# One block of attention products and sums per chunk, and chunk 0 through the same projection as the others, in a fused gated cross-attention and int8 feed-forward kernel

## What is computed

```
x = x + tanh(g_xattn) * ( softmax( q k^T / sqrt(32) ) v  @ Wo.T + bo )
        q = layernorm(x) @ Wq.T + bq         16 heads of 32
        k = ctx @ Wk.T + bk,  v = ctx @ Wv.T + bv
h  = gelu( qlinear(layernorm(x), w1, b1) )   512 -> 2048, int8 with one scale per tensor
x  = x + tanh(g_ffn) * qlinear(h, w2, b2)    2048 -> 512
```

## Time and profile before

| | |
|---|---|
| median of three runs | 603.9 us |
| the profiled execution | 603.55 us, its span 601.8 us |
| PE (TensorE matmul) busy | 577.0 us, 96% |
| DVE (VectorE) / ACT (ScalarE) / POOL busy | 457.9 (76%) / 338.7 (56%) / 246.5 us (41%) |
| granted TensorE clock over the run | 0.994 of full |

### The profile page before, as it was taken

One profiled execution on the slowest core, in us unless ns is written; L12 is line 12 of the kernel. 1 busy time (PEld: TensorE's weight loads), 2 busy tenths in 40 slices (PEclk: granted clock), 3 DMA queues, 4 the chain that ended last, 5 costly groups with the idle time before them and its releaser, 6 DMA issues. The chain is left out here.

```text
span 601.8 us, 9279 instructions
## 1 busy us (share of the span) xinstructions
PE 577.0 (96%) x3320; PEld 329.7 (55%) x3320; DVE 457.9 (76%) x658; ACT 338.7 (56%) x412; POOL 246.5 (41%) x211
## 2 busy tenths in 40 slices
PE   6999899999998999999999988999999999999997
PEld 5853656657566566585664763444444454444443
DVE  5865997868869788696795786889998799945182
ACT  1556274573763836628346536778776778445440
POOL 3268366464651764916062410000004529313383
PEclk8999999999999999999999999999999999999999
DMA  9926010320411403202001159677777967789766
GB/s 307 402 90 211 14 49 10 105 106 1 176 35 35 177 0 131 81 13 95 0 1 71 71 191 379 261 282 288 271 270 307 420 228 263 296 333 356 230 252 209
DMA packets 41223, 105.57 MB, mean 175 GB/s; under 512 B 3168, under 2 KB 3936, under 8 KB 36576
## 3 DMA queue, kind: packets, MB, share of 16 engines
q1 hardware_dynamic: 39840, 103.70, 46.6%
q10 hardware_dynamic: 1344, 1.37, 0.8%
HBM read 63.11 MB, written 41.94 MB: 175 GB/s over the span
## 5 line engine op out<-in xcount | busy, mean ns | idle before, releaser
L1466 PE MATMUL ps<-h_sb,w_q 128*128 (+1 forms) x488 | 111.3, 383 | 2.7 <-ACT xo L1533 2.6
L1765 PE MATMUL ps<-w_q,h_q 128*128 128x512 bf16 x448 | 96.9, 379 | 0.0
L1848 POOL TENSOR_TENSOR xo<-xo,b2s 128x512 f32<-128x512 f32 x32 | 52.6, 1675 | 70.8 <-DMA xo<-x_dram 52.7
L1466 PEld LDWEIGHTS ps<-h_sb,w_q 128*128 128x128 bf16 x488 | 46.9, 99 | 55.8 <-ACT xo L1533 3.9
L1765 PEld LDWEIGHTS ps<-w_q,h_q 128*128 128x128 bf16 x448 | 43.8, 98 | 52.9
L1533 ACT ACTIVATE xo<-ps,b1s,sc 128x1024 f32<-128x1024 f32 x48 | 57.7, 1205 | 26.0 <-PE ps L1466 17.9
L715 ACT ACTIVATE q_hi<-ps,bq_sb 128x512 fp32r<-128x512 f32 x32 | 22.0, 688 | 83.5 <-DVE ps L945 77.4
L729 ACT ACTIVATE prob<-ps 77x1024 f32<-77x1024 f32 x64 | 61.7, 1014 | 12.2 <-PE ps L474 12.2
L1633 DVE TENSOR_REDUCE hmax<-xo 128x1024 f32 (+1 forms) x48 | 57.1, 1213 | 7.8 <-ACT xo L1533 7.7
L1194 POOL TENSOR_TENSOR xt_lo<-xr,xt_hi 128x512 fp32r<-128x512 f32 x28 | 35.8, 1298 | 54.8 <-ACT xt_hi L708 54.7
L1825 DVE SCALAR_TENSOR_TENSOR xo<-ps,hs,xo 128x512 f32<-128x512 f32 x32 | 23.3, 746 | 40.7 <-POOL xo L1848 40.7
(11 more groups left out here) (187 smaller groups left out, 1118.2 us busy)
## 6 DMA issues: line engine op xcount, KB each, us to landing
h_dram<-xo SPq DMA_DIRECT2D x48, 512.0 KB, 2.8
h_sb<-h_dram SPq DMA_DIRECT2D x16, 1024.0 KB, 11.2
x_dram<-x SPq DMA_DIRECT2D x8, 1024.0 KB, 4.5
xo<-x_dram SPq DMA_DIRECT2D x8, 1024.0 KB, 4.9
x<-h_dram SPq DMA_DIRECT2D x8, 1024.0 KB, 7.9
x<-in_x SPq DMA_DIRECT2D x7, 1024.0 KB, 5.8
xr<-in_x_t SPq DMA_DIRECT2D x28, 256.0 KB, 2.9
out<-xo SPq DMA_DIRECT2D x7, 1024.0 KB, 8.4
```

The lines of the kernel that those rows point to most:

```text
L1466: mm = nc.tensor.matmul(ps[:, 2 * (m % 2) + s, :], w1_q[:, k, m * P:(m + 1) * P], xq_t[:, one(2 * j + s), k, :], start=(k == 0), stop=(k = ...
L1765: mm = nc.tensor.matmul(ps[:, 4 * s + t, :], h_q[s][:, m, t * P:(t + 1) * P], w2_q[:, m, :], start=(m == 0), stop=(m == MF - 1))
L1848: nc.gpsimd.tensor_tensor(xo[:, s, t, :], xo[:, s, t, :], b2s[:], ALU.add).then_inc(xb_on, 1)
```

## The change

Two parts.

**Chunk 0.** `normalize1`, `transposes`, `first_high`, `first_low` and the eight mean products are gone. TensorE starts with the column means, four products in plain float32 on the raw `Wq`; VectorE subtracts them straight from PSUM (`centre_wq`), and chunk 0 is projected like the others, from four loaded slices of transposed x in `xt0_raw`, first slices 0 and 1 for all four m, in banks 4 to 7. `split_k` and `split_wo` move from VectorE to POOL, the early loads are spread over SyncE's and ScalarE's queues, the idle turns ahead fall from 30 to 10. The load of w1 waits until the four `xt_lo` of chunk 0 are done.

**Chunks 1 to 6.** `SLOTS` is 8, and the products and sums of a whole chunk stand in step i+1 between `project_q(i+1, 0)` and `project_q(i+1, 1)`. In the last step the old order stays. `scores_by_key(i, 3)` moves behind the first 8 products of output tile 1. On ScalarE the four `c_copy` of the chunk stand around `q_high(i, 0)`; `centre2(i-2, 0)` moves from the end of the step before to behind them, beside `centre2(i-2, 1)`; `round_w1` comes next. On VectorE `amax2(i-2, 0)` and `(i-2, 1)` stand behind `q_low(i, 0)`, ahead of `reciprocals(i-1)`.

```diff
-SLOTS = 4
+SLOTS = 8
 @block.tensor
+                    for k in range(KD):
+                        pe.wait_ge(wq_in[k], 16)
+                        mm = nc.tensor.matmul(ps[:, MEAN_BANK, :], mean_w[:].to_broadcast([P, P]), wq_raw[:, k, :],
+                                              start=(k == 0), stop=(k == KD - 1))
...
                 def first_step():
...
+                    for k in range(2):
+                        for m in range(KD):
+                            first_q(m, [k])
+                    first_q(0, [2])
+                    for m in range(GROUPS):
+                        project_k(m)
+                    first_q(0, [3])
+                    row_turn(0)
+                    first_q(1, [2, 3])
+                    pe.wait_ge(k_split_hi, 4)
                     scores_by_token(0, 0)
+                    first_q(2, [2, 3])
+                    project_v(0, range(KD // 4))
                     scores_by_token(0, 1)
...
                 def step(i):
...
                     project_q(i, 0)
-                    values(i - 1, GROUPS - 1)
-                    sums(i - 1, GROUPS - 1)
+                    if in_one_block(i - 1):
+                        for g in range(GROUPS - 1):
+                            values(i - 1, g)
+                            sums(i - 1, g)
+                        sums(i - 1, GROUPS - 1)
+                        values(i - 1, GROUPS - 1)
+                    else:
+                        values(i - 1, GROUPS - 1)
+                        sums(i - 1, GROUPS - 1)
                     project_q(i, 1)
...
                     scores_by_key(i, 1)
-                    values(i, 0)
-                    sums(i, 0)
+                    if i == LAST:
+                        values(i, 0)
+                        sums(i, 0)
                     if older:
                         pe.wait_ge(x1_on, TT * (i - 2) + 3)
-                    project_out(i - 1, 0, 0, 3)
+                    project_out(i - 1, 0, 0, 3 if i == LAST else 9)
                     scores_by_key(i, 2)
...
-                    project_out(i - 1, 1, 0, 6 if i == LAST else ALL)
-                    values(i, 2)
-                    sums(i, 2)
+                    if i == LAST:
+                        project_out(i - 1, 1, 0, 6)
+                        values(i, 2)
+                        sums(i, 2)
+                    else:
+                        project_out(i - 1, 1, 0, 8)
+                        scores_by_key(i, 3)
+                        project_out(i - 1, 1, 8, ALL)
...
-                idle_turns(nc, sh, BS, 30)
-                transposes(0)
-                transposes(1)
-                project_k(0)
...
+                weight_means()
+                pe.wait_ge(ident_in, 16)
+                idle_turns(nc, sh, BS, 10)
 @block.scalar
...
-                    if c or p >= SLOTS:
-                        act.wait_ge(sum_mm, GROUPS * c + p // 2 - 1)
+                    if c and p == 0:
+                        act.wait_ge(sum_mm, GROUPS * c)
+                        act.wait_ge(av_mm, GROUPS * c)
...
+                    if in_one_block(i - 1):
+                        c_copy(i - 1, 0)
+                    q_high(i, 0)
+                    for g in range(1 if in_one_block(i - 1) else GROUPS - 1, GROUPS):
+                        c_copy(i - 1, g)
                     if older:
+                        centre2(i - 2, 0)
                         centre2(i - 2, 1)
+                    if 2 <= i < 2 + KD:
+                        round_w1(i - 2)
+                    for m in range(1, KD):
+                        q_high(i, m)
...
+                    exponentials(i, 6)
+                    exponentials(i, 7)
                     if older:
                         centre2(i - 2, 2)
                         centre2(i - 2, 3)
-                    exponentials(i, 6)
-                    exponentials(i, 7)
-                    centre2(i - 1, 0)
-                    c_copy(i, 2)
 @block.vector
...
                 def step(i):
                     older = i >= 2
-                    if older:
-                        amax2(i - 2, 1)
                     q_scale(i, 0)
                     q_low(i, 0)
+                    if older:
+                        amax2(i - 2, 0)
+                        amax2(i - 2, 1)
                     reciprocals(i - 1)
...
-                    if older:
-                        amax2(i - 2, 2)
-                        amax2(i - 2, 3)
                     if i == 1:
                         w1_scale()
...
-                    amax2(i - 1, 0)
+                    if older:
+                        amax2(i - 2, 2)
+                        amax2(i - 2, 3)
+                    if i == LAST:
+                        amax2(i - 1, 0)
```

More of the change, by code:

```diff
@@ L198, in attention @@
         idents_on = sem("idents_on")
+        mean_w_on = sem("mean_w_on")
+        xt0_in = [sem(f"xt0_in{k}") for k in range(KD)]
         k_zeroed = sem("k_zeroed")
@@ L294, in row_bank @@
         def row_bank(n):
-            return BS if n == 1 else BC
+            return (ROW0_BANK, W1)[n] if n < 2 else BC
         def rec_wide(g):
@@ L302, in rstd_value, with xt_tile @@
         def rstd_value(c):
-            return c + 2
+            return c + 1
+        def xt_tile(n, k):
+            return xr[:, k % 2, :] if n else xt0_raw[:, k, :]
         def xr_value(n, k):
@@ L384, in _ @@
             def _(pe):
[L385 to L391, removed]
                 def row_turn(n):
@@ L397, in row_turn @@
                         pe.wait_ge(c_on, GROUPS * (n - 1))
+                    elif n == 1:
+                        pe.wait_ge(v_on, B)
                     for t in range(TT):
@@ L1052, in first_step @@
                 def first_step():
+                    q_scale(0, 0)
                     q_low(0, 0)
[L1054 removed]
                     dve.wait_ge(max_zeroed, 1)
[L1056 to L1063 removed]
+                    for m in range(1, KD):
+                        q_scale(0, m)
+                        token_max(0, m - 1)
+                        q_low(0, m)
+                    token_max(0, 3)
                     dve.wait_ge(v_padded, 1)
                     dve.wait_ge(v_in, 48)
[L1066 removed]
                     add_bv(0)
[L1068 to L1069 removed]
+                    stats1(1)
                     add_bv(1)
@@ L1236, in add_bias, with split_k @@
                         pool.wait_ge(bog_on, 1)
-                        pool.wait_ge(xn_on, t + 1)
-                    else:
-                        pool.wait_ge(ln1_stats, TT * c + t + 1)
+                    pool.wait_ge(ln1_stats, TT * c + t + 1)
                     xa = x1[:, c * TT + t, :]
                     nc.gpsimd.tensor_tensor(xa, xa, sh.bo_gate[:], ALU.add).then_inc(xg_on, 1)
+                def split_k(b):
+                    if b:
+                        pool.wait_ge(ln1_rstd, rstd_value(batch(NC - 1) * NC // B + 1))
+                        pool.wait_ge(s_mm, PAIRS * (NC // B))
+                    src = sh.k_t1[:, :, :] if b else k_t[:, :, 0:NK]
+                    for r in range(4):
+                        pool.wait_ge(k_split_hi, 4 * b + r + 1)
+                        q = slice(DK * r, DK * (r + 1))
+                        hi = k_hi[q, :, :].bitcast(F32).rearrange("p (g r) n -> p g r n", r=4)[:, :, r, :]
+                        last = nc.gpsimd.tensor_tensor(k_lo[q, :, :], src[q], hi, ALU.subtract)
+                    last.then_inc(k_split, 1)
+                    pool.wait_ge(k_split, b + 1)
@@ L1243, in first_step, with split_wo @@
+                def split_wo(k):
+                    pool.wait_ge(w_hi_on, k + 1)
+                    nc.gpsimd.tensor_tensor(wo_lo[:, k, :], wo_raw[:, k, :], wo_hi[:, k, :].bitcast(F32),
+                                            ALU.subtract).then_inc(w_lo_on, 1)
                 def first_step():
-                    pool.wait_ge(k_biased, GROUPS)
+                    for k in range(KD):
+                        xt_low(0, k)
+                    rstd_1(0)
+                    split_k(0)
```

377 lines of the change are left out of this document (163 added, 214 removed).

## The result

The changed kernel took **641.56 us** (median of 4 runs, 637.38 to 643.78) beside 604.37 us for the kernel before on the same chip: a ratio of 1.063, with an interval of 1.059 to 1.066. The profiled execution took 643.78 us against 603.55, so 40.2 us are to be found between the two traces.

A forecast was written before the change was run, and what follows sets the result against it. TensorE's own instruction list was taken to bound the kernel from chunk 2 on. The terms -1.9 + 16.5 + 10.4 + 4.2 + 3.1 - 3.9 = +28.4 gave 632.0 us (632.3 beside the median), range 617 to 642.

The forecast's parts named there:

- The direction: Whole kernel: slower than before by more than 1%, chance 0.90.
- the two kinds of wait: TensorE waits for the maxima behind the late reciprocal, +16.5 us, and for low parts in output tile 0, +10.4 us.
- the clock: Behind the new long wait in steps 2 to 7: clock falls in two of six steps, +3.1 us, bounds 0 and 9.2.
- the start: Chunk 0: group 3's first values at 54.2 us instead of 58.13, -3.9 us, bounds -7.5 and +1.
- The reciprocal's wait: Steps 2 to 7: TensorE waits 2.75 us a step for maxima behind the late reciprocal, +16.5 us.
- Output tile 0's low parts: Steps 2 to 6: output starts before POOL's low parts are ready, three waits, 2.1 us a step, +10.4 us.
- K: Start of the scores by key of group 1; first low part was put at K + 2.6, wanted at K + 1.66.
- Step 1: Step 1: three low-part waits, 2.0 us, and one for w1's scale, 2.2 us: +4.2 us, bounds 2 and 5.
- the wait for w1's scale: Step 1, output tile 1: TensorE comes before VectorE has w1's scale and waits 2.2 us.
- denser work ahead of the wait: Long wait, steps 2 to 7: work ahead is denser than at the start, so falls in two of six, 3.1 us.
- rival 1: Long waits, steps 2 to 7: clock falls in all six, 9.2 us instead of 3.1, total 638 us; chance 0.15.
- Switches: Chunks 1 to 6: fewer changes between kinds of product on TensorE, about 0.1 us each, 0.3 a chunk, -1.9 us.

The follow-up runs named there:

- experiment 2: The changed kernel with 20 idle turns in TensorE's wait for the head maxima, steps 2 to 7: 633.19 us, ratio 1.048.
- experiment 1: The changed kernel with VectorE's reciprocal of chunk i-1 ahead of the two maxima of chunk i-2: 619.73 us, ratio 1.029.
- experiment 5: The changed kernel with the edits of experiment 1, experiment 3 and experiment 4 together: 609.10 us, ratio 1.011.
- experiment 6: Chunk 0 and the eight slots as changed, steps 1 to 7 in the order of the kernel before: 600.59 us, ratio 0.995.
- experiment 4: The changed kernel with group 0's values and sums back between the scores by key of group 1 and output tile 0: 629.28 us, ratio 1.045.
- experiment 3: The changed kernel with the copy of group 2 ahead of three centrings on ScalarE in the last step: 636.81 us, ratio 1.054.
- experiment 7: On experiment 6: eight small products ahead of the column means, and v's loads moved behind the gates': 599.68 us, ratio 0.994.
- experiment 9: On experiment 7: group 1's copy ahead of chunk 1's splits, and group 2's values and sums beside group 3's: 598.80 us, ratio 0.993.

## Why the prediction was right and wrong

The direction, the two kinds of wait and their places were right. The step that failed is the clock, which was put at 3.1 us and cost about 11; the last step's copy and the start were missed as well. The sum was +28.4 where the traces have +40.2. Where the experiments put a step's 6.29 us (44.78 against 38.49 with the old order):

| what | from | us a step |
|---|---|---|
| maxima ahead of the reciprocal, as a wait | 2 less 1 | 2.13 |
| clock behind that wait, where it falls | after less 2 | 1.57 |
| group 0 away from its place | 1 less 5 | 1.45 |
| left in 5: head maxima 0.45, low part once 0.47, rest of a block of three groups | 5 less 6 | 1.14 |

- **The reciprocal's wait: right.** Said 2.75 us a step from step 2 on. The products before it start at 109.02, the scores at 112.00, that is 2.75 more than the usual 0.23; six times as said. Moving its named cause behind the reciprocal took 2.13 of it. There the two maxima are still ahead of the first scaling, and 0.46 remains.
- **Output tile 0's low parts: right in kind, less as a wait.** Said 2.1 us a step, three waits. There are three, 0.39 + 0.73 + 0.29 = 1.41 us. POOL starts at 127.01 (said 127.02), but four low parts take 5.47 us in the run after against 5.54 for two pairs in the earlier trace rows, and TensorE has the first at 128.35, K + 2.20, where I had K + 2.6. Giving group 0 back its place saved 1.45 a step, so 7 us and not 10.4.
- **The clock: the step that failed.** I took a fall in two of six waits and 1.5 us each; it fell behind five, and it fell once more in step 1 and once behind the last step's wait. The price per fall was right (1.57 by experiment 2; in the change itself a step behind a wait with a fall takes 44.74 us, and one without takes 43.17). The number of falls was not: seven at about 1.6 are 11 us against 3.1, which is also near the growth of PE's busy time (11.7). That is 8 of the 11.8 us between the sum and the traces. Windows of the change, PE alone, behind the wait in step 2, in step 4, and in step 1:
```profile
112.00:116.00 4.00, 4.00 (x12) 0.58 0.00 0
202.50:206.00 3.50, 3.43 (x17) 1.00 0.00 0
...
87.20:91.00 3.80, 3.73 (x20) 0.71 0.41 126
```
  My reason against it, denser work ahead of the wait than at the start, carried nothing: the one row that had such a wait was the better guide. My rival 1 (638) priced it, with too small a chance. It was not exact either, since the clock held once in six here, three times in six in experiment 4 and twice in six in experiment 3. The Trainium skill ("TensorE: Matmul & The Clock Gate", section "HAM oscillation — how this bites in real kernels") describes a kernel that waited some 3 to 5 us for its data at every tile and started every tile at the lower clock. Here shorter waits, of 2.6 us, did it in most cases and not in all.
- **The last step: overlooked.** I counted the reciprocal's wait there but did not follow ScalarE's queue to its end, where the copy of group 2 stands behind three centrings. Experiment 3 took 3.5 us out of the last step by the traces, of 4.8 by the medians.
- **Step 4: overlooked, both ways.** Before, it was 2.5 us longer than its fellows. With k split on POOL, which I had not counted, 1.55 us of that are left in experiment 6. In the change TensorE waits 0.98 us for a copy that stands behind the rounding of k (1.85 us) on ScalarE.
- **Step 1: nearly right.** Said +4.2; the wait for w1's scale is 0.48 + 1.81 us against 2.2 said, the low parts 1.13 against 2.0. A clock of 0.71 behind four waits in a row comes on top: +6.1 like for like.
- **The start: mis-sized.** Said -3.9, measured -1.3. The means ended at 10.86 and not 9.3, since most of them ran at half pace: the median product instruction took 1061 ns, and 592 in experiment 7, where all eight together took 4.28 us behind the warm-up products. That this is the lower clock is only inferred: the granted clock of the stretch stands at 1.00 in the profile. Even in 7 they cost more than the 3.6 us of my sum. Besides, wk had landed only by 20.1 and kept TensorE idle for 1.08 us ahead of the k projection, and the scores came at 28.91 against 25.9. ScalarE's four castings ahead of `q_high(0, 0)` were as said.
- **Switches: right and small.** One block less a step is 0.12 us by experiment 9, where I had 0.1 for one switch and so 0.2 for a block. A saving of this size never stood a chance against one wait of 2.6 us.

## What to carry to other kernels

When work is gathered into one block, look at what each queue now has between the block and its next consumer, on every engine and in the last iteration too: here two short maxima ahead of a 3.35 us reciprocal, three centrings ahead of a copy and a missing 1.8 us of other work cost 32.5 of the 37.2 us, while one block less in a step is worth 0.12. Where TensorE has no slack, price a new wait of 2.6 us at itself plus 1.6 for the clock, unless runs show otherwise. Time won at the start is not kept by itself: in experiment 6 step 1 took back 1.3 us of 1.7.

## What the runs showed of the hardware

- The same wait, 2.55 to 2.59 us of idle TensorE behind the same products, lowered the clock in 12 of 18 cases (five of six in the change, three of six in experiment 4, four of six in experiment 3). In these kernels the windows of about 4 us behind it have a clock of 0.54 to 0.69 where it fell. The idle time alone does not decide it, and I found no row that does.
- Behind the last step's wait of 2.81 or 2.82 us the clock fell in the change (0.57 over 4 us) and in experiment 4 (0.63), and held at 1.00 in experiment 1.
- The clock also fell behind short waits, and not always. In the change's step 1, four of 0.72, 0.41, 0.48 and 1.81 us between 80.28 and 87.27 us were followed by 0.71; nearly the same four (0.73, 0.42, 0.46 and 1.81 us) left it at 1.00 in experiment 3. In experiment 5, 1.81 us behind a single short wait of 0.47 were followed by 0.63. Window of that kernel (PE alone):
```profile
87.40:92.00 4.60, 4.58 (x24) 0.63 0.38 109
```
- 20 idle turns in the wait (2.35 us of work, 0.41 us of idle time left) kept the clock at 1.00 behind all six such waits in experiment 2.
- VectorE's reciprocal of 128x512 takes 3.35 us, where the scaling, an operation on two operands of that shape, takes 0.68.
- Steps in the old order take 38.49 us with the eight slots and 38.64 without; the cause stays open.
